# A diffuser loop on one core: bias taken into the matmul, statistics read from PSUM, q and v ahead of the transposed q

## What is computed

```python
def _diffuser(x, ref, qv_w, k_w, proj_w, proj_b, ln_g, ln_b):
    k = (ref @ k_w)...                                     # 10 references
    for _ in range(STEPS):                                 # 3
        q, v = (x @ qv_w)...                               # 12 heads of 16
        attn = einsum('bhnd,rhmd->brhnm', q, k) * scale
        attn = einsum('brhnm,brhkm->brhnk', attn, attn)
        o = einsum('brhnk,bhkd->brhnd', attn, v).reshape(B, NB_REF, N, C)
        x = mean(o.transpose(0, 2, 3, 1), axis=-1)
        x = layernorm(x @ proj_w + proj_b) * ln_g + ln_b
    return x
out = correct_m * corrected + (1.0 - correct_m) * xm
```

## Time and profile before

| | us |
|---|---|
| median of 3 runs (542.62 to 555.36) | 547.23 |
| the profiled execution | 549.04 |
| its span, from first to last instruction | 547.2 |
| PE busy | 445.6 (81%) |
| DVE busy | 318.5 (58%) |
| ACT busy | 237.0 (43%) |
| POOL busy | 220.9 (40%) |

### The profile page before, as it was taken

The page is one execution under the profiler, slowest core; times in us unless marked ns, Lnnn a source line. Parts: engine busy times, 40 slices in busy tenths (PEclk is TensorE's granted clock), DMA queues, the critical chain, the costliest instruction groups (busy, mean ns, idle before and its releaser), DMA issues.

```text
span 547.2 us, 13333 instructions
## 1 busy us (share of the span) xinstructions
PE 445.6 (81%) x4370; PEld 352.7 (64%) x4370; DVE 318.5 (58%) x912; ACT 237.0 (43%) x687; POOL 220.9 (40%) x334
## 2 busy tenths in 40 slices
PE   3992588799999965489999998763299999999975
PEld 3972545466666544389898897663287677676764
DVE  1110323388888888687878877545466556565523
ACT  0130324365555532277666654401265554555403
POOL 1000003345545547545446744355334534445214
PEclk9996587799999995567667867555589999999988
DMA  8609513454545541000000000002211111110023
GB/s 265 221 11 323 192 45 74 120 126 108 118 116 122 110 104 18 2 1 3 1 4 14 13 15 14 13 25 85 65 45 46 42 26 41 28 31 21 11 75 121
DMA packets 52161, 38.46 MB, mean 70 GB/s; under 512 B 36187, under 2 KB 45541, under 8 KB 51328
## 3 DMA queue, kind: packets, MB, share of 16 engines
q1 hardware_dynamic: 48832, 26.89, 19.1%
q10 hardware_dynamic: 1008, 7.15, 4.0%
q0 software_dynamic: 2256, 3.57, 2.0%
HBM read 24.00 MB, written 14.33 MB: 70 GB/s over the span
## 4 chain that ended last, share of the span: by engine, by line
PE 61%; DVE 12%; issue 9%; POOL 6%; DMA 4%; ACT 3%; ACTq 3%; SPq 2%; POOLq 0%; DVEq 0%
PE wide L358 29%; PE bank L358 25%; PE bank L363 3%; ACTq L706 3%; PE bank L545 2%; POOL rstd L1222 2%; DVE xs L895 2%; ACT xT L801 2%; POOL srt_dram L1249 1%; PE bank L621 1%; DMA bdm<-in_bdm 1%; DVE rm L985 1%; PE wide L545 1%; DVE xT L993 1%; DMA xT<-in_w 1%
## 5 line engine op out<-in xcount | busy, mean ns | idle before, releaser
L1295 POOL DMA_INDIRECT y_dram<-qkbm,ydst x25 | 25.8, 1032 | 70.7 <-PE bank L358 27.3
L691 ACT ACTIVATE xT<-wide 108x384 f32<-108x384 f32 (+1 forms) x70 | 26.0, 407 | 60.1 <-PE wide L358 44.9
L895 DVE TENSOR_SCALAR xs<-yb,mv,rstd 108x192 f32<-108x192 f32 x24 | 43.5, 1814 | 5.4 <-POOL rstd L1222 5.0
L358 PE MATMUL bank<-xT 108*32 108x96 f32 (+4 forms) x629 | 32.3, 265 | 16.5 <-ACT xT L691 10.7
L358 PEld LDWEIGHTS bank<-xT 108*32 108x32 f32 (+4 forms) x629 | 24.1, 143 | 33.2 <-issue 21.3
L724 ACT ACTIVATE xT<-bank,gains 96x128 f32<-96x128 f32 (+1 forms) x72 | 28.7, 454 | 38.4 <-PE bank L621 31.9
L358 PE MATMUL bank<-wqv,xTs 128*108 128x384 f32 x96 | 41.0, 554 | 3.4 <-DVE xT L993 3.4
L1167 DVE CAST xs<-xT 128x384 f16<-128x384 f32 x50 | 21.6, 431 | 35.7 <-ACT xT L855 34.7
L358 PE MATMUL wide<-w2h,xs 128*128 x300 | 41.9, 248 | 0.4
L1249 POOL DMA_INDIRECT srt_dram<-row,dst x22 | 22.8, 1037 | 42.0 <-DVE dst L1050 34.0
L1221 POOL TENSOR_SCALAR veps<-mv 108x1 f32<-108x1 f32 x46 | 10.7, 232 | 70.8 <-DVE mv L889 70.2
(11 more groups left out here) (230 smaller groups left out, 1283.1 us busy)
## 6 DMA issues: line engine op xcount, KB each, us to landing
srt_dram<-row ACTq DMA_DIRECT2D x8, 800.2 KB, 10.4
xT<-in_xT SPq DMA_DIRECT2D x11, 324.0 KB, 6.6
xT<-srt_dram SPq DMA_DIRECT2D x25, 97.0 KB, 2.0
hT<-in_w SPq DMA_DIRECT2D x8, 288.0 KB, 3.2
xT<-in_w SPq DMA_DIRECT2D x8, 288.0 KB, 3.2
xT<-in_w SPq DMA_DIRECT2D x4, 576.0 KB, 4.0
hT<-in_w SPq DMA_DIRECT2D x4, 576.0 KB, 3.8
scratch<-xT SPq DMA_DIRECT2D x72, 27.0 KB
```

Source lines behind the costliest of these rows:

```text
L358: return nc.tensor.matmul(o, l, r, start=start, stop=stop)
L691: return nc.scalar.activation(o, i, ACT.Copy)
L895: return V.tensor_scalar(o, x, mv[0:rows, n % 4, 0:1], r[0:rows, n % 4:n % 4 + 1], ALU.subtract, ALU.mult)
L1295: G.indirect_dma_start(y_dram, bass.IndirectOffsetOnAxis(ydst[:, q:q + 1], 0), ysb[:, q % YB], None, bounds_check=2 * NTOK - 1, oob_is_err ...
```

## The change

1. The projection's bias `attn_proj_b` becomes row 96 of the padded weight `wpa`, and row 96 of `ocT` is set to one. `vecs` loses a vector (5 to 4).
2. DVE doesn't move y to `yb` any more. Statistics and normalisation read bank 1, in the iteration of y itself; `y_read` is now signalled by the normalisation, which waits for POOL's `std_ready`.
3. PE has qv ahead of qT, and DVE has `vm` at the head of the iteration, ahead of the copies of qT.

The core of the diff (left out: line counts of `vecs`, the host's `vec` list, `turned = {}`):

```diff
@@ PE, to_features(i) @@
-                pe.wait_ge(S["xs_ready"], i + 1)
+                if i < MT:
+                    pe.wait_ge(S["xs_ready"], i + 1)
+                else:
+                    pe.wait_ge(S["y_read"], i - MT + 1)
...
                     pe.wait_ge(S["xT_ready"], i + 1)
                     if i >= 1:
+                        pe.wait_ge(S["qp_ready"], i)
+                        pe.wait_ge(S["vm_ready"], i)
+                    for k in range(2):
+                        last = mm(bank[2][0:T, 0:2 * C], xTs[:, i % 2, k, :], wqv[:, k, :], k == 0, k == 1)
+                    last.then_inc(S["qv_psum"], 1)
+                    if i >= 1:
                         pe.wait_ge(S["qT_ready"], i)
...
                     last.then_inc(S["qT_psum"], 1)
-                    if i >= 1:
-                        pe.wait_ge(S["qp_ready"], i)
-                        pe.wait_ge(S["vm_ready"], i)
-                    for k in range(2):
-                        last = mm(bank[2][0:T, 0:2 * C], xTs[:, i % 2, k, :], wqv[:, k, :], k == 0, k == 1)
-                    last.then_inc(S["qv_psum"], 1)
@@ ACT, from_turn(i) @@
-                    act.wait_ge(S["qv_psum"], i - 1)
+                    act.wait_ge(S["qT_psum"], i - 1)
@@ DVE @@
-            V.memset(ocT[HF:], 0.0).then_inc(S["pad_ready"], 1)
+            link(V.memset(ocT[HF:], 0.0))
+            V.memset(ocT[HF:HF + 1, 0], 1.0).then_inc(S["pad_ready"], 1)
...
                 if i < NI:
+                    dve.wait_ge(S["qp_ready"], i + 1)
+                    if i >= 2:
+                        dve.wait_ge(S["r_psum"], i - 1)
+                    V.tensor_tensor(vm[:, i % 2], bank[2][0:T, C:2 * C][:, None, :].broadcast_to([T, JB, C]),
+                                    rowm[:, 0:JB, None].broadcast_to([T, JB, C]), ALU.mult).then_inc(S["vm_ready"], 1)
                     dve.wait_ge(S["qT_psum"], i + 1)
...
-                if i >= 6:
-                    last = i - 6
-                    dve.wait_ge(S["std_ready"], turned[last] + 1)
-                    dve.wait_ge(S["xT_psum"], last + 1)
-                    if last < NI - MT:
-                        centred(xs[:, last % MT], yb[:, last % 2], turned[last]).then_inc(S["xs_ready"], 1)
-                    else:
-                        link(centred(xs[:, last % MT], yb[:, last % 2], turned[last]))
-                        link(V.tensor_tensor(xs[:, last % MT], xs[:, last % MT], vec(V_ALG), ALU.mult))
-                        link(V.tensor_tensor(xs[:, last % MT], xs[:, last % MT], vec(V_ALB), ALU.add))
...
                 if 0 <= p < NI:
+                    y = bank[1][0:T, 2 * T:2 * T + C]
                     dve.wait_ge(S["y_psum"], p + 1)
-                    V.tensor_tensor(yb[:, p % 2], bank[1][0:T, 2 * T:2 * T + C], vec(V_APB), ALU.add).then_inc(S["y_read"], 1)
-                if i < NI:
-                    dve.wait_ge(S["qp_ready"], i + 1)
-                    V.tensor_tensor(vm[:, i % 2], bank[2][0:T, C:2 * C][:, None, :].broadcast_to([T, JB, C]),
-                                    rowm[:, 0:JB, None].broadcast_to([T, JB, C]), ALU.mult).then_inc(S["vm_ready"], 1)
-                if 0 <= p < NI:
-                    dve.wait_ge(S["y_read"], p + 1)
-                    turned[p] = moments(yb[:, p % 2])
+                    turned = moments(y)
+                    dve.wait_ge(S["std_ready"], turned + 1)
+                    dve.wait_ge(S["xT_psum"], p + 1)
+                    centred(xs[:, p % MT], y, turned).then_inc(S["y_read"], 1)
+                    if p >= NI - MT:
+                        dve.wait_ge(S["y_read"], p + 1)
+                        link(V.tensor_tensor(xs[:, p % MT], xs[:, p % MT], vec(V_ALG), ALU.mult))
+                        link(V.tensor_tensor(xs[:, p % MT], xs[:, p % MT], vec(V_ALB), ALU.add))
@@ host @@
+    wpa = padded(a["attn_proj_w"])
+    wpa[HF, 0] = a["attn_proj_b"]
```

More of the change, by code:

```diff
@@ L52 @@
 BAR = 2.0 ** 15
-V_TOKB, V_APB, V_ALG, V_ALB, V_FPB = range(5)
+V_TOKB, V_ALG, V_ALB, V_FPB = range(4)
 G_DIFF, G_LN1, G_LN2 = range(3)
@@ L72, in vit_kernel @@
         tokw = sb("tokw", [128, KF, C])
-        vecs = sb("vecs", [T, 5, C])
+        vecs = sb("vecs", [T, 4, C])
         gains = sb("gains", [HF, 3, 2, 2])
@@ L953, in normalise @@
                 centred(h1[:, t], src, first[t]).then_inc(S["h1_ready"], 1)
-            turned = {}
             for i in range(NI + 6):
@@ L1335 @@
             qkbm[1, :, :, HD + 3 * u + j] = np.where(image == j, np.float32(-BAR), np.float32(0))
-    vec = [a["tok_b"], a["attn_proj_b"], a["attn_ln_g"], a["attn_ln_b"], a["ffn_proj_b"]]
+    vec = [a["tok_b"], a["attn_ln_g"], a["attn_ln_b"], a["ffn_proj_b"]]
     gains = [[a[ln + "_g"], a[ln + "_b"]] for ln in ("attn_ln", "ffn_ln1", "ffn_ln2")]
@@ L1348 @@
         "tokw": a["tok_W"].reshape(C, KF, 128).transpose(2, 1, 0),
-        "vecs": np.broadcast_to(np.stack(vec)[None], (T, 5, C)),
+        "vecs": np.broadcast_to(np.stack(vec)[None], (T, 4, C)),
         "gains": np.stack([np.stack(g) for g in gains]).reshape(3, 2, 2, HF).transpose(3, 0, 1, 2),
@@ L1355 @@
         "wq": padded(a["attn_qv_w"][:, :C]), "wqT": halves(a["attn_qv_w"][:, :C].T),
-        "wpa": padded(a["attn_proj_w"]),
+        "wpa": wpa,
         "wqkvp": np.stack([halves(wqkp[:, 0]).reshape(HF, -1), halves(wqkp[:, 1]).reshape(HF, -1),
```

## The result

The changed kernel takes 568.68 us (median of 4 runs, 568.13 to 571.55), beside 548.09 us for the kernel before on the same chip: a ratio of 1.042, 95% interval 1.033 to 1.051. It is slower.

A forecast was written before the change was run, and what follows sets the result against it. PE was taken to bound the loop, VectorE some iterations through contention with GpSimd. 7.7 (iterations 7 to 23) + 6.9 (0 to 6) + 4.3 (drain) = +18.9 us: 567.9 profiled, 566.1 as median; range 552 to 577.

The forecast's parts named there:

- The bias row at nothing: Bias as a row of the padded product, vecs one row shorter, one more memset: costed at nothing.
- The period: Middle of the loop: y waits for ACT's copy of q, vm, qT copies; 5.27 us, 5.59 with w2, against 4.79.
- The two places where iterations 7 to 23 differ from the sum: Additions to the 91.5 us: +1.5 for scaling h in iterations 7 to 10; +0.6 and +0.3 in iterations 22 and 23.
- The scaling of h: ACT scales h between xTs and the weight piece in iterations 7 to 10: 0.37 us each, +1.5 us.
- rival (c): In the loop PE falls to its lower clock for longer, two iterations at half speed: 573 us; chance 0.11.
- The normalisation from PSUM: In the loop on VectorE: 0.38 us from PSUM, not blocked by GpSimd; bounds 0.25 and, if still blocked, 1.80.
- Rival (d): Loop: the split still blocks the normalisation from PSUM, qT waits, period 6.0 (6.8): 581 us; chance 0.05.
- The head of the loop: Iterations 0 to 6: y(0) waits behind vm and copies, delaying a later weight piece; +6.9 us, bounds 0.9 and 10.
- the slip of 0.9 in iteration 4: Two pieces in iteration 4 make o(3), its store and later pieces about 0.9 us late; q copied at 105.0, not 104.13.
- The drain: Iteration 24 to L1014: VectorE's and GpSimd's parts no longer lie side by side; 32.7 us, +4.3, bounds -3.6 and +7.
- (a): Loop: PE keeps its pace if q's copy comes by T+1.9, so y would not wait: 539 us; chance 0.07.
- (b): Only the loop's period grows (+7.7 us), weight pieces' arrival and drain having unseen slack: 555 us; chance 0.15.

The follow-up runs named there:

- the two runs that cut it at either end: Changed kernel with `vm` put back behind rm on VectorE: 552.86 us (1.009); changed kernel with q' copied first on ScalarE: 550.22 us (1.004).
- the run without splits: Changed kernel with GpSimd computing only 8 columns of each weight piece's low half: 559.73 us, one run.
- the two made from it that keep both orders: Changed kernel with GpSimd's low halves left out but for 8 columns: 559.73 us; changed kernel with the last pass's normalisation in two parts: 555.69 us.
- the statistics from PSUM alone: Changed kernel with both orders put back (qT ahead of qv on PE, `vm` behind rm on VectorE): 588.06 us, ratio 1.072.
- the kernel before without splits: Kernel before with GpSimd computing only 8 columns of each weight piece's low half: 543.5 us, one run.
- two-part normalisation alone: Changed kernel; last pass does (y - mean) x gain from PSUM without rstd, then x rstd + bias an iteration later: 555.69 us, ratio 1.016.
- the fastest: Changed kernel with `vm` behind rm, q' copied first on ScalarE, and the last pass's normalisation in two parts: 539.43 us, ratio 0.985.

## Why the prediction was right

566 us was forecast with a range of 552 to 577, and 568.7 was measured; for the profiled execution 567.9 was summed, and 569.07 came. The other 1.4 us between the medians are that the forecast took the median 1.8 us below the profiled execution, as in the kernel before, and it was 0.4 below. By its steps:

**The bias row at nothing:** right, shown by the run of it alone (1.001).

**The period.** 5.27 and 5.59 were forecast; 5.25 and 5.57 are what the starts show (184.80 to 190.05, and 190.05 to 195.62 with the w2 piece). The steps from the iteration's start at T = 184.80: piece at T+1.59 (forecast 1.60), q' at 2.33 (2.35), `vm` at 2.69 (2.71), copies done at 3.80 (3.82), y at 3.90 (3.87). That this chain and no other makes the period is shown by the two runs that cut it at either end, both 4.87. Between 110 and 200 us the view of waits gives `vm` 26.1 us of idle VectorE ahead of it:

```profile
DVE xT L965 <- ACT xT L694: 26.1, 16, 5.9
```

(total, times, longest). The normalisation's new wait for rstd is 1.00 in iteration 19 above (the steps up to rstd and rstd itself are those of the earlier trace rows); qv on PE covers it, since y is released at T+1.62 and qT starts at T+1.76.

**The two places where iterations 7 to 23 differ from the sum.** 93.9 us was forecast, 94.4 measured. Iterations 22 and 23 took 6.02 each where 5.87 and 5.9 were in the sum, and the one at 7 took 6.25, with PE's clock low behind the idle time ahead of it (windows of the changed kernel, columns as above):

```profile
118.00:124.70 6.70, 6.49 (x56) 4.47 (x48) 2.49 (x9) 3.12 (x8) 2.46 (x3) 0.74 0.52 127
...
125.00:205.00 80.00, 69.62 (x644) 46.52 (x642) 37.25 (x116) 40.58 (x108) 40.11 (x45) 1.00 0.46 104
```

The scaling of h cost less than the 0.37 in the sum (iterations 9 and 10 took 5.51 and 5.50). So rival (c) happened in one iteration and not in several: from 125 to 205 us PE kept its full clock, though it waited in every iteration.

**The normalisation from PSUM.** 0.38 was taken, between 0.25 and 1.80; it is 0.477, the same in all 24 executions, with a split beside it or not. The mechanism was right and the size was off by 0.1, which is hidden under qv. Rival (d) fell by this row. The rule cited there from the Trainium skill (SBUF — State Buffer, "Who interferes with whom") agrees with the rows: the normalisation with its input in PSUM is not held by the split (475 to 478 ns), and the gain with two inputs in SBUF is held (357 undisturbed, up to 2111). That the split is the cause of the second is shown by the run without splits (357 to 359).

**The head of the loop.** +6.9 was forecast, +6.7 measured; iteration 7 was to start at 118.7 and does at 118.50. Timeline of iterations 5 and 6, which answers to the earlier trace rows:

```profile
103.66 0.31 ACT L694 ACTIVATE xT<-bank 108x192 f32<-108x192 f32 x1
104.00 0.76 DVE L965 TENSOR_TENSOR xT<-bank,rowm 108x576 f32<-108x576 f32 x1 [9.93 <-ACT xT L694]
...
105.25 1.58 PE L358 MATMUL bank<-wpa,ocT 128*108 128x192 f32 x4 [7.31 <-DVE xT L971]
...
110.41 0.83 SPq L329 DMA_DIRECT2D hT<-in_w  x2
...
113.72 0.84 ACT L694 ACTIVATE w1h<-hT 96x768 f16<-96x768 f32 x1 [4.02 <-DMA hT<-in_w]
...
118.50 0.59 PE L363 MATMUL bank<-ident,xT 108*96 108x108 f32 x2
```

y(0) stands behind `vm` and so behind a piece from DRAM (7.31 us idle), o(4) and its store stand behind y(0), and the request for the next piece behind that store in SP's queue: the piece arrives at 113.72 where it had come at 110.39. The steps hold, but not every number in them. q' was copied at 103.66 where 105.0 was put, so the slip of 0.9 in iteration 4 is not to be seen. The way from the next piece's copy to iteration 7 made up for it (118.50-113.72 = 4.8 us, and 118.7-115.1 = 3.6 in the sum), mostly because y and o ran at the lower clock once more (y 1.59 us). So that the head came out within 0.2 us is in part luck: one number was 1.3 us too late, another 1.2 too short. The pieces themselves come at other times in each profile (the w2 piece of iteration 5 between 98.3 and 103.2 us over the ten kernels), so the firmer measure is the distance from that copy to iteration 7: 8.72 us before and in the run with the bias row alone, 15.91 in the changed kernel, 15.91 and 15.70 in the two made from it that keep both orders, and 8.74 with `vm` behind rm, where y(0) runs at 96.83, before that piece is copied. By it the head costs 7.2. It comes from `vm` at the head together with a late q', as in the middle of the loop: with `vm` at the head and q' copied first it is 6.17. (It is 11.76 with the statistics from PSUM alone, where PE stands idle for 6.18 us ahead of a qT in iteration 6 until the normalisation is done, and qT and qv then run at the lower clock; and 7.13 in the kernel before without splits, so splits have a share of the head too.)

**The drain** is the term that was sized worst: +4.3 forecast, +5.7 measured. Its mechanism is right but for the gain that it named: PE was no longer to stand for rm(23), and it still stood for 2.02 of the 3.59 us, because the gain beside a split now holds rm. The steps: the first normalisation at T+10.0 (9.6 forecast), then 7.7, 8.4 and 6.4 us (7.5, 8.3 and 5.9), and 1.6 (1.4). Each step was a little short, by 0.1 to 0.5, and all on one side. That they hang on the splits and on waiting for rstd is shown by two runs: without splits the drain is 28.1, without PE's wait for rstd 25.7.

**Behind the loop** nothing was forecast, and 320.2 against 320.8 us came. This stretch took between 316.9 and 327.7 us in the ten kernels (last section), so that it came out the same is luck as well.

**The rivals.** (a) falls by q' at T+2.33, where it asked for T+1.9; (b) by the head and the drain, which both grew.

## What to carry to other kernels

An engine that is half idle can still set the period by the order of its program: before an instruction is moved ahead on an in-order engine, ask when its input comes and who waits for what it is moved past. Taking work from such an engine (38 us here) need not buy anything, while a wait that the same edit turns into a round trip over another engine (statistics, rstd on GpSimd, normalisation, bank free) must be covered by work of the engine behind it, in the ordinary iterations and in the drain, where no such work is left. Where a bank is held only until a scale is known, do first the part that doesn't need the scale.

## What the hardware showed

- With a wait of 1.35 us in every 6.34 us iteration PE was not at its full clock in six of 17 iterations (qv 2.56 instead of 1.54 us). With 0.5 us of waiting in 5.25 it stayed full. I had priced PE's waits in that kernel at their length only.
- The normalisation out of PSUM takes 477 ns, out of SBUF undisturbed 380: dearer at rest, and cheaper than the 1799 that the latter took in the median beside GpSimd.
- The stages behind the loop took 316.9 to 327.7 us in the profiled executions, though no edit touches them. Windows of their first 80 us, of the kernel with the shortest (two-part normalisation alone) and with the longest (kernel before without low halves):

```profile
233.00:313.00 80.00, 71.75 (x1059) 66.90 (x1060) 66.11 (x203) 53.90 (x187) 44.13 (x95) 0.78 0.02 6
```

```profile
214.00:294.00 80.00, 73.83 (x959) 71.20 (x960) 62.15 (x176) 51.02 (x170) 40.02 (x88) 0.65 0.01 4
```

The granted clock there is 0.78 in the one and 0.65 in the other, and PE gets through 1059 records against 959. So the clock probably has a part in the difference; that it has, and how much, was not shown. The kernels between the two don't line up so well (0.67 goes with 320.8 in the kernel before, 0.71 with 324.9 in the fastest). The long stretch behind its loop is why the kernel before without splits reaches the next block 12.4 us earlier (214.05 against 226.42) and has a span only 5.5 us shorter. What sets this clock stays open.
